# The first block's 32 table lookups, made in two rounds of 32 and of 96 rows

## What is computed

```python
e = jnp.stack([tbl_0[ids[:, 0]], tbl_1[ids[:, 1]], ..., tbl_31[ids[:, 31]]], axis=1)   # 1024 x 32 x 16
x0 = h = e
for i in range(3):                                # W0: 128 x 1024; W1, W2: 128 x 2048
    z = (x0[:, :, None, :] * h[:, None, :, :]).reshape(B, F * G, E)
    y = relu(einsum('oc,bce->boe', Ws[i], z) + bs[i][None, :, None])
    if i != 2:
        x_keep, h = y[:, :64, :], y[:, 64:, :]
    else:
        x_keep, h = y, y
    xs.append(x_keep)
z = sum(concatenate(xs, axis=1), axis=2)          # 1024 x 256
h = concatenate([z, dense_ctx], axis=1)
h = maximum(h @ W_top1 + b_top1, 0); h = maximum(h @ W_top2 + b_top2, 0)
y = h @ W_top3
```

## Time and profile before

| what | us |
|---|---|
| median of 2 runs (1050.23 to 1051.23) | 1050.73 |
| span of the profiled execution, first to last instruction | 1048.4 |
| PE busy in that span | 1008.3 |
| DVE busy | 826.9 |
| POOL busy | 815.7 |
| ACT busy | 476.5 |

### The profile page before, as it was taken

One profiled execution on the slowest core, in us unless ns is written; L12 is line 12 of the kernel. 1 busy time (PEld: TensorE's weight loads), 2 busy tenths in 40 slices (PEclk: granted clock), 3 DMA queues, 4 the chain that ended last, 5 costly groups with the idle time before them and its releaser, 6 DMA issues.

```text
span 1048.4 us, 11722 instructions
## 1 busy us (share of the span) xinstructions
PE 1008.3 (96%) x3269; PEld 589.9 (56%) x3269; DVE 826.9 (79%) x757; ACT 476.5 (45%) x600; POOL 815.7 (78%) x524
## 2 busy tenths in 40 slices
PE   3788999999999999999999999999999999999988
PEld 3744555555555555555555555555555555555555
DVE  4466777898788977898789977897889977788882
ACT  2143544444444544444544544444444544443443
POOL 7658789887998789887989799887989765556640
PEclk9998999999999999999999999999999999999999
DMA  7099999888998888889998889888998888889000
GB/s 160 10 208 220 204 197 198 191 193 187 211 202 189 192 186 190 192 188 191 199 207 185 196 186 191 190 190 189 197 205 187 195 188 190 183 189 227 21 1 1
DMA packets 48629, 184.15 MB, mean 176 GB/s; under 512 B 17442, under 2 KB 22050, under 8 KB 28132
## 3 DMA queue, kind: packets, MB, share of 16 engines
q1 hardware_dynamic: 40420, 181.83, 79.1%
q0 software_dynamic: 8192, 2.11, 1.9%
HBM read 180.75 MB, written 3.15 MB: 175 GB/s over the span
## 4 chain that ended last, share of the span: by engine, by line
POOL 45%; PE 25%; issue 16%; DMA 7%; DVE 3%; ACT 2%; POOLq 0%; SPq 0%; ACTq 0%; DVEq 0%
POOL low L514 25%; POOL looked_up L504 17%; PE y L643 15%; PE y L651 6%; DMA looked_up<-in_tbl,ids_now 4%; PE y L666 3%; POOL tail_parts L522 2%; DVE unsplit L1117 1%; DMA spread<-xcols 1%; DMA xcols<-xrows 1%; DVE prod L1117 1%; DMA shifted<-xcols 1%; ACT emb L828 0%; ACT tail_high L888 0%; ACT tail L887 0%
## 5 line engine op out<-in xcount | busy, mean ns | idle before, releaser
L514 POOL TENSOR_TENSOR low<-unsplit,high 128x1024 fp32r<-128x1024 f32 x221 | 524.7, 2389 | 104.8 <-ACT high L864 103.2
L643 PE MATMUL y<-prod,w1T 128*128 128x512 f32 x1024 | 478.4, 595 | 2.5 <-ACT kept L856 2.1
L1117 DVE TENSOR_TENSOR prod<-spread,h 128x1024 f32<-128x1024 f32 x288 | 348.9, 1215 | 118.0 <-PE y L643 102.3
L864 ACT CAST high<-unsplit 128x1024 fp32r<-128x1024 f32 x224 | 234.0, 1045 | 238.0 <-DVE unsplit L1117 237.6
L1117 DVE TENSOR_TENSOR unsplit<-spread,h 128x1024 f32<-128x1024 f32 x224 | 271.9, 1214 | 46.1 <-ACT h L850 46.0
L504 POOL DMA_INDIRECT looked_up<-in_tbl,ids_now x256 | 248.4, 970 | 67.2 <-issue 57.5
L643 PEld LDWEIGHTS y<-prod,w1T 128*128 128x128 f32 x1024 | 192.8, 191 | 162.2 <-issue 140.0
L651 PE MATMUL y<-high,w2T_high 128*128 128x512 f32 x448 | 226.9, 506 | 4.3 <-ACT high L864 4.3
L666 PE MATMUL y<-low,w2T_high 128*128 128x512 f32 x448 | 202.5, 533 | 5.0 <-POOL low L514 4.7
L850 ACT ACTIVATE h<-y,bias 64x512 f32<-64x512 f32 x128 | 83.3, 651 | 210.9 <-PE y L643 210.1
L651 PE MATMUL y<-high,w2T_low 128*128 128x512 f32 x448 | 177.8, 397 | 0.0
(11 more groups left out here) (119 smaller groups left out, 468.9 us busy)
## 6 DMA issues: line engine op xcount, KB each, us to landing
spread<-xcols SPq DMA_DIRECT2D x128, 1024.0 KB, 9.1
shifted<-xcols SPq DMA_DIRECT2D x120, 256.0 KB
shifted_tail<-xcols SPq DMA_DIRECT2D x120, 64.0 KB
looked_up<-in_tbl,ids_now POOLq DMA_INDIRECT x256
xcols<-xrows SPq DMA_DIRECT2D x32, 96.0 KB, 2.0
spread<-in_L_rec_W SPq DMA_DIRECT2D x3, 512.0 KB, 7.2
spread<-in_L_rec_W SPq DMA_DIRECT2D x1, 1024.0 KB, 11.4
wt<-in_W_top SPq DMA_DIRECT2D x2, 512.0 KB, 8.3
```

The lines of the kernel that those rows point to most:

```text
L514: pool.tensor_tensor(low[kind][r][:, :, :], unsplit[kind][r][:, :, :], high[kind][r][:, :, :].bitcast(F32), ALU.subtract).then_inc(s_low[k ...
L643: last = pe.matmul(y[:, :], w, z[:, c, :], start=(n == 0 and c == 0), stop=(item in (LAST0, LAST1) and c == ITEM - 1))
L864: act.copy(high[kind][r][:, :, :], unsplit[kind][r][:, :, :]).then_inc(s_high[kind], 1)
L1117: dve.tensor_tensor(z, x[:, ITEM * n:ITEM * (n + 1), :], b[:, :].unsqueeze(1).to_broadcast([P, ITEM, COLS]), ALU.mult).then_inc(s_made[kin ...
```

## The change

The first block's 32 lookups become 64: one round that fetches the rows of partitions 0 to 31 from all 32 tables, and then one that fetches the rows of partitions 32 to 127. An indirect transfer takes its ids from as many partitions as it has rows, so the second round's ids come from a tile of their own, `ids_rest`, whose 96 partitions begin at 0; SP loads it by a transfer of its own, ahead of the first weights. POOL waits for it between the rounds. As `s_looked` now gets 32 times 16 more, the waits on it in `begin` and in `take_rows` count one block more. Nothing is taken up before both rounds have landed: ACT still copies all of `looked_up` at once.

```diff
--- before.py
+++ after.py
@@ -51,6 +51,7 @@
 XROWS = FIELDS + FIELDS // 2
 DENSE = 16
 COPY = 32
+FIRST_ROWS = 32
 
 IDLE_TURNS, IDLE_LOOPS = 8, 16
 
@@ -223,6 +224,7 @@
         ids_sb = sb("ids_sb", [P, BLOCKS, FIELDS], I32)
 
         ids_now = sb("ids_now", [P, FIELDS], I32)
+        ids_rest = sb("ids_rest", [P - FIRST_ROWS, FIELDS], I32)
         emb, emb_at = sb_at("emb", [P, FIELDS, EMBED])
         looked_up = sb("looked_up", [P, FIELDS, EMBED])
 
@@ -284,6 +286,7 @@
         prep = [bank[:, :].rearrange("p (a b) -> p a b", b=P) for bank in y2]
 
         s_ids = sem("s_ids")
+        s_ids_rest = sem("s_ids_rest")
         s_w0 = sem("s_w0")
         s_w1 = sem("s_w1")
         s_w2 = sem("s_w2")
@@ -380,6 +383,7 @@
         @block.sync
         def _(sp):
             sp.dma_start(ids_sb[:, :, :], ids.rearrange("(n p) f -> p n f", p=P)).then_inc(s_ids, 16)
+            sp.dma_start(ids_rest[:, :], ids[FIRST_ROWS:P, :]).then_inc(s_ids_rest, 16)
             sp.dma_start(w0_raw, w0[:, :]).then_inc(s_w0, 16)
 
             ALL, MORE = FIELDS * HALF, (CHUNKS + WRAP - FIELDS) * HALF
@@ -496,7 +500,7 @@
 
             def begin(b):
 
-                pool.wait_ge(s_looked, 16 * FIELDS * b)
+                pool.wait_ge(s_looked, 16 * FIELDS * (b + 1))
                 pool.wait_ge(s_emb, b)
                 next_ids(b)
 
@@ -549,7 +553,16 @@
 
             next_ids(0)
             for f in range(FIELDS):
-                look_up(f)
+                pool.indirect_dma_start(
+                    out=looked_up[0:FIRST_ROWS, f, :], out_offset=None, in_=tables[f][:, :],
+                    in_offset=bass.IndirectOffsetOnAxis(ap=ids_now[0:FIRST_ROWS, f:f + 1].bitcast(U32), axis=0),
+                ).then_inc(s_looked, 16)
+            pool.wait_ge(s_ids_rest, 16)
+            for f in range(FIELDS):
+                pool.indirect_dma_start(
+                    out=looked_up[FIRST_ROWS:P, f, :], out_offset=None, in_=tables[f][:, :],
+                    in_offset=bass.IndirectOffsetOnAxis(ap=ids_rest[:, f:f + 1].bitcast(U32), axis=0),
+                ).then_inc(s_looked, 16)
             begin(1)
             for f in range(LOOKUPS_BEFORE_TAIL):
                 look_up(f)
@@ -824,7 +837,7 @@
             def take_rows(t):
 
                 b = t[0] + t[1] // TILES_PER_BLOCK
-                act.wait_ge(s_looked, 16 * FIELDS * (b + 1))
+                act.wait_ge(s_looked, 16 * FIELDS * (b + 2))
                 act.copy(emb[:, :, :], looked_up[:, :, :]).then_inc(s_emb, 1)
 
             def repeat_fields(t):
```

## The result

The changed kernel takes 1087.88 us (2 runs, 1087.78 to 1087.99) against 1050.73 us, 1.0355 times as long, 95% interval 1.0336 to 1.0374. The forecast was 1088.0 us, between 1068 and 1095. The profiled execution spans 1086.0 us, 37.6 us more than before.

What follows compares the result with a forecast made beforehand. The prediction took the first block's run of lookups on POOL to bound the head, PE most of the span. Added lookups 36.7 us plus PE's clock 0.6 make 37.3, taking the median from 1050.7 to 1088.0 us, range 1068 to 1095.

Steps and rivals of the forecast that it cites:

- The price of the rows: In POOL's lookups: 128 rows cost 0.10 us, as 128 elements of a plain fill do; 3.2 us off the sum.
- the upper end: First block's lookups: the added time lies near 39.9 us, at 36.7, since 32 rows make as many packets as 128.
- All of it goes to the end: First block's lookups on POOL: everything later hangs on them, so a microsecond more or less there is one at the end.
- The ids' transfer: On SP ahead of the weights: delays them about half a microsecond, hidden under the lookups; nothing, without this cover 0.5 us.
- the register instruction: One more in ACT's and POOL's loops: below 0.1 us each, counted as nothing.
- DVE's sums on the first round: Sums added 1.9 us to two lookups before; they hold up other ones as much now, give or take 1.9 us.
- The last landing: From the last lookup's start to its landed rows before ACT's copy: 2.34 us, to stay as it is.
- PE's clock: First tile after PE's longer idle time: restart at half clock, 0.6 us counted, at most 3 us.
- Rows as the cost: Rival on the lookups: 32 and 96 rows cost little more than 128; adds 9.6 to 13.1 us; chance 0.14.
- half and half: Rival on the lookups: about 0.45 us of the 0.947 go by rows; adds 25 us, 1076; chance 0.2.
- a step paced by transfers: Rival on the lookups: the rows' transfer, not POOL, sets the step; 1051 us, no change; chance 0.03.
- the upper bound: First block's lookups: rows cost nothing, each of 32 added instructions costs a full step of 0.947 + 0.30; 39.9 us.

Runs made afterwards that it cites:

- the fills: Kernel before, whole lookups kept, plus 34 POOL fills of an idle tile that ACT's first copy waits for; 1083.41 us against 1050.23.
- the ids first: Kernel before, first block's ids loaded by their own transfer straight into the tile lookups read, without POOL's copy; 1050.14 us against 1050.48.
- PE kept at work: Changed kernel with 57 loops of idle turns on PE in place of 16; 1088.37 us, against 1050.23 for the kernel before.
- four rounds: All 32 tables looked up in rounds of 32 rows, 128 instructions against 32 in the kernel before; 1158.83 us against 1050.23.
- the sums in pieces: Kernel before with each of DVE's two first sums cut into 8 of 128x128; 1051.00 us against 1050.06.
- half the tables: Tables 0 to 15 looked up twice by parts, tables 16 to 31 by whole lookups; 1075.19 us against 1050.23 for the kernel before.
- one table in two rounds: Only table 0 looked up in two parts, 33 lookups in the first block; 1049.31 us against 1050.48 for the kernel before.

## Why the prediction was right, point by point

- **Each added lookup costs its instruction, not its rows.** Forecast 36.7 us, measured 36.4 at the first copy. The price of the rows, 0.10 us for 128, taken from two plain fills, is 0.107 us by the line through three sizes. That is luck: no run shows that a lookup's rows and a fill's elements have anything in common. The reason given for the upper end, the 32 packets of each lookup whatever its size, holds as a count; that the packets are what costs isn't shown. Nor do all of them carry rows: by their sizes in the traces of before and after, 16 of the 32 hold rows (512 bytes in a whole lookup, 128 and 384 in the two rounds) and 16 hold 4 bytes. The Trainium skill ("DMA: Bandwidth & Descriptors", Rules for kernel authors) advises against two transfers to disjoint partition halves, as they serialize on the DMA engines that they share. The outcome agrees, though not the reason: the DMA engines were 0.06 busy from 48 to 80 us, and what was paid is POOL's time, 1.14 us for each added lookup.
- **All of it goes to the end.** Shown by the fills for a delay: 32.1 us at the copy, 32.1 at the end. For a gain ("a microsecond more or less") it isn't: with the ids first, the copy came 2.3 us earlier and the end 2.2 us later in the profiled execution, and the medians are the same (1050.14 and 1050.48 us).
- **The ids' transfer, the wait for it, the register instruction: nothing.** The first two are shown by their run. The last was not tried alone. The half microsecond by which the weights were to come later doesn't show: DVE's first sum starts at 6.28 us, before at 6.71, and over all the runs between 5.58 and 9.11.
- **DVE's sums on the first round: as before.** The two lookups lost 1.67 us (1.01 + 0.66), against 1.9.
- **The last landing stays.** 2.11 us from the last lookup's start to its rows, 0.23 less.
- **PE's clock, +0.6 us: wrong in what it does at the end.** It fell as expected, and cost 2.1 us on the second tile. But the second block's copy stood where it would have stood without that. The step that failed is that a loss on the first tile lasts: the transfers, which the prediction names among PE's waits, take back all of it, and not a part. The run with PE kept at work shows that the term is 0.
- **What made up for it was not foreseen**: POOL's pauses. In the changed kernel POOL stands still for 3.93 us behind the copy of the fourth block's ids:

```profile
285.06 0.21 POOL L495 COPY ids_now<-ids_sb 128x32 int32 x1
289.20 0.98 POOL L508 DMA_INDIRECT looked_up<-in_tbl,ids_now  x1 [3.93 <-issue]
```

  The shift goes from 36.3 to 39.1 us there. The kernel before has its longest pause ahead of its 227th lookup (the 0.16 us behind a `split_low` is usual):

```profile
722.44 7.05 POOL L514 TENSOR_TENSOR low<-unsplit,high 128x1024 fp32r<-128x1024 f32 x3
730.71 0.96 POOL L504 DMA_INDIRECT looked_up<-in_tbl,ids_now  x1 [1.23 <-issue]
```

  The changed kernel has none at the same place:

```profile
761.14 7.04 POOL L518 TENSOR_TENSOR low<-unsplit,high 128x1024 fp32r<-128x1024 f32 x3
768.34 0.96 POOL L508 DMA_INDIRECT looked_up<-in_tbl,ids_now  x1 [0.16 <-issue]
```

  That gives 1.3 us back (38.7 to 37.4). So the 37.6 us are 36.4, less 0.1 up to the third copy, 2.8 more by the pause, less 0.4 bit by bit, less 1.3, and 0.2 more in the last tiles; the forecast was 36.7 + 0.6. Its total fits closer than its terms do, which is luck: the 0.6 us stood for something that doesn't last, and 1.2 us came from something else. Of the terms of this sum, the 2.8 us are repeated by five kernels (2.7 to 2.9 us at copy 4 in four, 2.0 at copy 2 with four rounds). The 1.3 us depend on how long the pause before happened to be, and the smaller ones are read from one pair of executions.
- **Rivals.** Rows as the cost, half and half, and a step paced by transfers are excluded by 867 and 920 ns with gaps of 0.30; the upper bound, 39.9 us with rows that cost nothing, by the 53 ns between the two. A higher price for odd sizes does exist (120 rows), though not for 32 and 96. Two side sums are off: 9.6 to 13.1 us are 0.9% to 1.2%, and 42 us more end at 1093 us, within the range and not over 1095.

## What to carry to other kernels

An indirect lookup on POOL is priced by the instruction: in this kernel of a millisecond, 32 more of them on a path that nothing covers are 36 to 40 us in the splits tried, though no more rows are fetched. Before splitting a transfer into rounds, ask what starts earlier for it; here nothing did, since the reader still waited for all of it. And when a path's head is shortened, look at what was put in to fill the time, such as idle turns: it can become the path.

## What the runs showed of the hardware

- An indirect lookup of n rows of 64 bytes held POOL for 0.84 us and 0.83 ns a row at 32, 96 and 128 rows, with 0.30 us to the next; 64 rows took 0.903 us, 8 rows 0.863, and 120 rows 0.982, more than 128.
- A lookup that started while DVE was adding two SBUF tiles ended 0.82 us after the end of a sum (0.76 us with 32 rows); sums that follow at once kept one out for 3.69 us, though the one before it had got in between two of them. The Trainium skill, "SBUF — State Buffer", Who interferes with whom, says that a DVE instruction with two SBUF inputs contends with a GpSimd instruction that reads SBUF. A lookup reads its ids from there, and the run with the sums in pieces agrees.
- POOL pauses for up to 6.04 us ahead of some lookup, at places that repeat: ahead of the 129th with 3.93 or 3.94 us in all five kernels with 64 or more lookups of under 128 rows, and there ahead of the 242nd again (0.21 to 0.26 us); ahead of the 128th and the 241st with half the tables; ahead of the 114th (0.21 to 0.68 us) and the 227th (0.44 to 1.47) in the seven kernels with whole lookups alone, also with 34 fills and as many waits more in POOL's program. From one pause to the next there are 113 whole lookups in all of these; with one table in two rounds there is one ahead of the 115th, and none ahead of the 228th. So it goes by the lookups made so far, not by the length of the program or by time. What POOL does in it, how long it takes and what sets the first place stay open: neither the number of the lookups nor the count of their rows alone gives 114, 115, 128 and 129, and no run took it apart further.
